# Linear attention's output pass moved into the next element's middle, with narrower key-value, numerator and score products

## The reference, cut to what matters

```python
qkv = xn @ Wqkv                     # 128 -> 3 x 1024
q, k = elu(q) + 1, elu(k) + 1       # exp below zero, t + 1 above
kv = einsum('bhnd,bhnf->bhdf', k, v)
k_sum = k.sum(axis=-2)
out = einsum('bhnd,bhdf->bhnf', q, kv) / (einsum('bhnd,bhd->bhn', q, k_sum) + 1e-6)
s = out.reshape(B, N, 1024) @ Wout + bout
```

## Time and profile before

| What | Value |
|---|---|
| median of three runs | 2235.43 us |
| profiled execution, its own time | 2234.39 us |
| its span | 2232.6 us |
| PE busy | 1934.6 us (87%), 17956 records |
| PEld busy | 1381.8 us (62%) |
| DVE busy | 1362.9 us (61%) |
| ACT busy | 1096.1 us (49%) |
| POOL busy | 214.6 us (10%) |
| mean granted TensorE clock | 0.953 |

### The profile page before, as it was taken

How to read it: one execution, slowest core, us unless ns; L and a number is a source line. 1 busy time by engine, 2 the same in 40 slices (tenths; PEclk the granted TensorE clock), 3 DMA queues, 4 the chain that set the end, 5 groups by cost and what they waited for, 6 DMA issues and landing times.

```text
span 2232.6 us, 50773 instructions
## 1 busy us (share of the span) xinstructions
PE 1934.6 (87%) x17956; PEld 1381.8 (62%) x17972; DVE 1362.9 (61%) x3678; ACT 1096.1 (49%) x2434; POOL 214.6 (10%) x235
## 2 busy tenths in 40 slices
PE   6999999998999999959888988898988899898652
PEld 4666666666666666636667566765766676666552
DVE  6666666666666666637665765577666566755312
ACT  3444444443555445425665465555555554555332
POOL 0000000000000000030011001101111110010022
PEclk9999999999999999969999999999999999999887
DMA  3222222222122211230221112110211111111374
GB/s 127 79 87 87 87 87 92 91 86 64 59 68 68 67 49 53 75 116 23 63 67 47 56 56 66 52 30 24 67 46 58 58 53 41 37 46 42 124 233 119
DMA packets 97041, 159.05 MB, mean 71 GB/s; under 512 B 14279, under 2 KB 65607, under 8 KB 93640
## 3 DMA queue, kind: packets, MB, share of 16 engines
q1 hardware_dynamic: 87720, 134.93, 18.7%
q0 software_dynamic: 9248, 23.17, 3.4%
HBM read 96.35 MB, written 61.69 MB: 71 GB/s over the span
## 4 chain that ended last, share of the span: by engine, by line
PE 59%; DVE 20%; ACT 7%; issue 7%; SPq 3%; DMA 2%; POOL 1%; another core or an unknown queue 1%; DVEq 0%; ACTq 0%; POOLq 0%
PE psum L1032 5%; PE psum L870 5%; PE psum L937 4%; PE psum L830 4%; PE psum L764 3%; PE psum L1012 3%; PE psum L987 3%; PE psum L1142 3%; PE psum L952 2%; PE psum L1090 2%; PE psum L959 2%; PE psum L786 2%; PE psum L904 2%; PE psum L1041 2%; PE psum L877 2%
## 5 line engine op out<-in xcount | busy, mean ns | idle before, releaser
L1349 ACT ACTIVATE pts<-psum 128x512 f32<-128x512 f32 x192 | 99.1, 603 | 201.1 <-PE psum L904 201.1
L1803 DVE TENSOR_REDUCE mneg<-psum 128x2 f32<-128x512 f32 (+1 forms) x192 | 119.1, 683 | 46.8 <-PE psum L885 25.1
L671 POOL DMA_INDIRECT rows<-h,recA x64 | 61.5, 961 | 894.7 <-DVE recA L1585 767.3
L786 PE MATMUL psum<-txT,wt 128*128 128x128 f32 x864 | 118.9, 281 | 32.1 <-ACT txT L1241 32.0
L786 PEld LDWEIGHTS psum<-txT,wt 128*128 128x128 f32 x864 | 106.7, 194 | 43.9 <-ACT txT L1241 38.4
L870 PE MATMUL psum<-wa,xT_s 128*128 128x512 f32 x256 | 118.0, 603 | 2.6 <-DVE mneg L1803 2.6
L1032 PE MATMUL psum<-xT_s,wa 128*128 128x256 f32 x512 | 116.6, 381 | 0.0
L695 POOL DMA_INDIRECT rows<-xn,recC x32 | 31.5, 983 | 861.5 <-DVE recC L2007 741.3
L1550 DVE TENSOR_TENSOR tg<-tg,psum 128x256 f32<-128x256 f32 x84 | 35.2, 419 | 113.6 <-ACT tg L1230 109.2
L1032 PEld LDWEIGHTS psum<-xT_s,wa 128*128 128x128 f32 x512 | 95.8, 192 | 12.9 <-issue 1.0
L795 PE MATMUL psum<-wt,tg 128*128 128x128 f32 x528 | 79.2, 280 | 14.6 <-DVE tg L1552 13.8
(11 more groups left out here) (272 smaller groups left out, 4862.7 us busy)
## 6 DMA issues: line engine op xcount, KB each, us to landing
wt<-in_wB SPq DMA_DIRECT2D x84, 384.0 KB, 2.9
outs<-pbd SPq DMA_DIRECT2D x16, 1024.0 KB, 7.2
wt<-in_wD SPq DMA_DIRECT2D x24, 578.0 KB, 3.5
wa<-in_wD SPq DMA_DIRECT2D x15, 578.0 KB, 3.6
tx<-rows SPq DMA_DIRECT2D x132, 64.0 KB, 2.9
outs<-ty SPq DMA_DIRECT2D x132, 64.0 KB, 1.6
rows<-pbd SPq DMA_DIRECT2D x64, 128.0 KB, 1.7
rows<-pbd SPq DMA_DIRECT2D x8, 1024.0 KB, 3.9
```

What stands on the lines that cost most here:

```text
L786: last = mm(bank(f"th{j}")[:, c * P:(c + 1) * P], view[s][:, c * P:(c + 1) * P], txT[:, s, :], start=True, stop=True)
L1349: af(pT[:, n, :], bank(f"e{n}"), ACT.Exp, scale=float(HD) ** -0.5).then_inc(*frees(f"e{n}"))
L1803: ins = v.tensor_reduce(mneg[:, int(n >= 4), col:col + hs], sc, AX.X, ALU.max, negate=True)
```

## The change

The products of keys with values and the numerators are computed per head: 64 weight columns and 65 moving columns for keys with values, blocks of 64 rows by 64 columns for the numerators. `kvb` halves to 65 columns, and the two heads of a pair sit in its lower and upper 64 partitions. They take two banks for four. The masks of `scores(1)` and `scores(2)` cover only the second 128 keys, and each of their products is cut into two of 128 keys.
The transposes of the linear outputs (`outputs_turned`), their copies by ScalarE and the output product s0 (`linear_output`) are no longer done at the end of the same element: they are stage G's, so they run for the element before, in the middle of the present one. In "GP" they run once more, behind the gate. `oT` moves from the keys' buffer to the one that the exponentials of the queries had. In VectorE's order the sum of s0 with the bias stands between `divided(0)` and `divided(1)`; the wait for the stored record moves to x2. The load of three layer-1 weights by SyncE waits for s0 of "GP".
Left out below: the same calls in the order for segments without A, the counts of `PER`, and the removed ScalarE helper that comes back unchanged but for its first two lines.

```diff
@@ -91,20 +91,23 @@
         names += [f"sc{n}" for n in range(4, 8)]
-        names += [f"kv{j}" for j in range(4)]
+        over("oT00", "oT01")
+        names += [f"kv{j}" for j in range(2)]
         tile_step(2)
+        over("oT10", "oT11")
         names += [f"num0{j}" for j in range(4)]
+        over("s0")
         tile_step(4)
-        names += ["oT00", "oT01", "pn0", "pd0", "oT10", "oT11"]
+        names += ["pn0", "pd0"]
         tile_step(5)
-        names += ["pn1", "pd1", "s0"]
+        names += ["pn1", "pd1"]
@@ -249,7 +251,7 @@
         reg = sb("reg", [P, 12 * 512])
-        kvb = sb("kvb", [P, NP, 2 * V0])
+        kvb = sb("kvb", [P, NP, V0])
@@ -320,7 +322,7 @@
         o_tok = big[:, 2 * INNER + NT * H * V0:].rearrange("p (t f) -> p t f", t=NT)
-        oT = big[:, 0:2 * INNER].rearrange("p (a n) -> p a n", a=NP)
+        oT = reg[:, 0:2048].rearrange("p (a n) -> p a n", a=NP)
@@ -330,7 +332,7 @@
         diag_mask = cmask[:, 1:2, :].to_broadcast([P, GR, P])
-        row_mask = cmask[:, 0:2, :].rearrange("p (o t) n -> p o (t n)", o=1).to_broadcast([P, 2, N])
+        diag_mask_2 = cmask[:, 1:2, :].to_broadcast([P, 2, P])
@@ -594,6 +596,7 @@
                     sp.wait_ge(*given("h2_ready"))
+                    sp.wait_ge(*read_out("s0"))
@@ -860,6 +863,27 @@
+            def outputs_turned(t):
+                if "G" not in now["stages"]:
+                    return
+                pe.wait_ge(*given("o_ready", t - 1))
+                for c in range(2):
+                    pe.wait_ge(*emptied(f"oT{t}{c}"))
+                    for a in range(4):
+                        last = tr(bank(f"oT{t}{c}")[:, a * P:(a + 1) * P], o_tok[:, t, (4 * c + a) * P:(4 * c + a + 1) * P])
+                    last.then_inc(*fills(f"oT{t}{c}"))
+            def linear_output():
+                if "G" not in now["stages"]:
+                    return
+                pe.wait_ge(*emptied("s0"))
+                pe.wait_ge(*read_out("oT11"))
+                for t in range(NT):
+                    for pr in range(NP):
+                        last = mm(bank("s0")[:, t * P:(t + 1) * P], oT[:, pr, t * P:(t + 1) * P], wout0[:, pr, :], start=(pr == 0), stop=(pr == NP - 1))
+                last.then_inc(*fills("s0"))
@@ -874,7 +898,10 @@
                         pe.wait_ge(*emptied(use))
-                        mm(bank(use), identb[:, :], diag_mask if part == 0 else row_mask, start=True, stop=False)
+                        if part == 0:
+                            mm(bank(use), identb[:, :], diag_mask, start=True, stop=False)
+                        else:
+                            mm(bank(use).rearrange("p (h n) -> p h n", h=2)[:, :, P:N], identb[:, :], diag_mask_2, start=True, stop=False)
@@ -882,7 +909,9 @@
                             else:
-                                last = mm(bank(use)[:, a * N:(a + 1) * N], qr[p0:p0 + HD, 2 * (part - 1) + a, P:N], kr[p0:p0 + HD, :], start=False, stop=(a == heads - 1))
+                                for kt in range(NT):
+                                    last = mm(bank(use)[:, a * N + kt * P:a * N + (kt + 1) * P], qr[p0:p0 + HD, 2 * (part - 1) + a, P:N], kr[p0:p0 + HD, kt * P:(kt + 1) * P],
+                                              start=False, stop=(a == heads - 1 and kt == NT - 1))
@@ -906,23 +935,21 @@
                     if t == 0:
-                        for j in range(4):
+                        for j in range(2):
                             pe.wait_ge(*read_out(f"kv{j}"))
+                    for hh in range(2):
+                        for c in range(2):
+                            pe.wait_ge(*emptied(f"num{t}{2 * hh + c}"))
                         pe.sem_inc(sem("tiles_open"), 1)
-                    for j in range(4):
-                        pe.wait_ge(*emptied(f"num{t}{j}"))
-                        for a in range(2):
-                            pr = 2 * j + a
-                            last = mm(bank(f"num{t}{j}")[:, a * N:a * N + 2 * V0], qt[:, pr, t * P:(t + 1) * P], kvb[:, pr, :], start=True, stop=True)
-                        last.then_inc(*fills(f"num{t}{j}"))
-                def outputs_turned(t):
-                    pe.wait_ge(*read_out(f"num{t}3"))
-                    for c in range(2):
-                        pe.wait_ge(*emptied(f"oT{t}{c}"))
                         for a in range(4):
-                            last = tr(bank(f"oT{t}{c}")[:, a * P:(a + 1) * P], o_tok[:, t, (4 * c + a) * P:(4 * c + a + 1) * P])
-                        last.then_inc(*fills(f"oT{t}{c}"))
+                            for ch in range(2):
+                                tokens = slice(t * P + ch * CH, t * P + (ch + 1) * CH)
+                                for c in range(2):
+                                    rows = slice(c * DH, (c + 1) * DH)
+                                    last = mm(bank(f"num{t}{2 * hh + c}")[ch * CH:(ch + 1) * CH, a * V0:(a + 1) * V0], qt[rows, 4 * hh + a, tokens],
+                                              kvb[rows, 4 * hh + a, :], start=True, stop=True)
+                                    if a == 3 and ch == 1:
+                                        last.then_inc(*fills(f"num{t}{2 * hh + c}"))
@@ -976,22 +1003,26 @@
                 scores(1)
+                outputs_turned(0)
                 pe.wait_ge(*read_out("v11"))
-                for j in range(4):
-                    pe.wait_ge(*emptied(f"kv{j}"))
-                    for a in range(2):
-                        pr = 2 * j + a
+                for hh in range(2):
+                    pe.wait_ge(*emptied(f"kv{hh}"))
+                    for a in range(4):
                         for t in range(NT):
-                            last = mm(bank(f"kv{j}")[:, a * N:a * N + 2 * V0], k_tok[:, t, pr * P:(pr + 1) * P],
-                                      v_tok[:, t, 2 * pr:2 * pr + 2, :], start=(t == 0), stop=(t == NT - 1))
-                    last.then_inc(*fills(f"kv{j}"))
+                            for c in range(2):
+                                hd = 2 * (4 * hh + a) + c
+                                last = mm(bank(f"kv{hh}")[c * DH:(c + 1) * DH, a * V0:(a + 1) * V0], k_tok[:, t, hd * DH:(hd + 1) * DH],
+                                          v_tok[:, t, hd, :], start=(t == 0), stop=(t == NT - 1))
+                    last.then_inc(*fills(f"kv{hh}"))
                 tile_step(2)
+                outputs_turned(1)
                 numerators(0)
+                linear_output()
@@ -1000,17 +1031,9 @@
                 tile_step(4)
-                outputs_turned(0)
                 weighted(0)
-                outputs_turned(1)
                 weighted(1)
-                pe.wait_ge(*emptied("s0"))
-                pe.wait_ge(*read_out("oT11"))
-                for t in range(NT):
-                    for pr in range(NP):
-                        last = mm(bank("s0")[:, t * P:(t + 1) * P], oT[:, pr, t * P:(t + 1) * P], wout0[:, pr, :], start=(pr == 0), stop=(pr == NP - 1))
-                last.then_inc(*fills("s0"))
@@ -1322,6 +1348,18 @@
+            def outputs_turned(t):
+                if "G" not in now["stages"]:
+                    return
+                act.wait_ge(*given("q0_ready", 1 if "A" in now["stages"] else 0))
+                act.sem_inc(sem("act_turn"), 1)
+                for c in range(2):
+                    act.wait_ge(*filled(f"oT{t}{c}"))
+                    src = bank(f"oT{t}{c}").rearrange("p (a n) -> p a n", a=4)
+                    ins = af(oT[:, 4 * c:4 * c + 4, t * P:(t + 1) * P], src, ACT.Copy)
+                    ins.then_inc(*frees(f"oT{t}{c}"))
@@ -1782,6 +1815,14 @@
+            def linear_output():
+                if "G" not in now["stages"]:
+                    return
+                dve.wait_ge(*filled("s0"))
+                v.tensor_tensor(s0[:, :, :], tok(bank("s0")[:, 0:N]), boutb[:, :].rearrange("p (o d) -> p o d", o=1).to_broadcast([P, NT, D]), ALU.add).then_inc(*frees("s0"))
+                dve.wait_ge(*read_out("s0"))
@@ -1824,17 +1865,19 @@
                             dve.wait_ge(*filled(f"num{t}{j}"))
-                            nm = bank(f"num{t}{j}").rearrange("p (a n) -> p a n", a=2)[:, :, 0:2 * V0].rearrange("p a (h v) -> p a h v", v=V0)
-                            den = dn[:, 4 * (j % 2):4 * (j % 2) + 4].rearrange("p (a h) -> p a h", a=2)
-                            v.tensor_scalar(den, nm[:, :, :, DH], 1e-6, None, ALU.add).then_inc(*signals("dve_chain"))
+                            nm = bank(f"num{t}{j}")[:, 0:4 * V0].rearrange("p (a v) -> p a v", v=V0)
+                            den = dn[:, 4 * (j % 2):4 * (j % 2) + 4]
+                            v.tensor_scalar(den, nm[:, :, DH], 1e-6, None, ALU.add).then_inc(*signals("dve_chain"))
                         for j in (2 * pair, 2 * pair + 1):
-                            nm = bank(f"num{t}{j}").rearrange("p (a n) -> p a n", a=2)[:, :, 0:2 * V0].rearrange("p a (h v) -> p a h v", v=V0)
```

(28 more changed lines are left out.)

23 lines of the change are left out of this document (12 added, 11 removed).

## The result

| What | Before | After |
|---|---|---|
| median of 19 runs each | 2238.62 us (2228.66 to 2242.86) | 2250.16 us (2236.7 to 2264.99) |
| profiled execution, its own time | 2234.39 us | 2250.16 us |
| its span | 2232.6 us | 2248.2 us |
| PE busy | 1934.6 us | 1925.0 us |
| DVE busy | 1362.9 us | 1340.8 us |

The ratio of the times is 1.0053, with a 95% interval of 1.0033 to 1.0074. The change makes the kernel some 12 us slower, where 20 us less was forecast. The 2250 us lie inside the forecast's range of 2180 to 2256, near its slow end, but the direction is the other one. TensorE has 10 us less of busy time although it works slower on average, so work was saved. The last row of the table is where to look.

The account below looks back on a forecast made before the run. TensorE's order of work, with a few stops ended by VectorE, was taken to bound the layer-0 loops. First loop -9, tiled elements -7, first element -6.5 and "GP" +2.5 made -20 us: 2214 us, range 2180 to 2256.

Parts of the forecast that it names:

- Keys with values: Layer 0's key-value products, now 64 narrower records at 33 ns: 2.1 us, 1.7 less per element.
- rival C: Narrow key-value products don't overlap in the column halves, 59 ns each: +27 us on the forecast, 2241 us; chance 0.17.
- Numerators: Per token half, 16 records become 64 quadrant records: 1.05 us for 1.9, 0.85 less, twice per element.
- The stall: Middle: VectorE idle some 3 us before the maxima's transpose, TensorE 1.9 and 1.1 us; 2 to 3.5 in the tail.
- ScalarE's open late start: Tail, first loop: ScalarE starts 1.6 us after the weighted sums, unexplained; taken as 0.1 to 1.6 us.
- The whole at full clock: Per element without clock loss: 3.8 us less in the first loop, 3.0 us less with tiles.
- The first element: No predecessor, so its transposes and output product vanish; middle 2.6 us earlier, tail 5.8 less with 2.0 open: -6.5 us.
- Clock: First loop: one fall of the old length, 1.7 us lost, plus 1.0 for the tail wait; net -1.1 per element.
- tiled elements: Elements with expert tiles: -3.0 us at full clock, +2.0 for a new clock fall, -1.0 times 7 = -7 us.
- Rival B: Output product ahead of the maxima's transpose stalls VectorE, then TensorE; two clock falls per element: +21, 2256 us; chance 0.18.
- Rival A: The clock holds, because output product and transposes fill the middle enough: -55, 2179 us; chance 0.15.
- Layer 1: The loops behind 1020 us, left aside because nothing of the diff runs there; no term in the sum.

Follow-up runs that it names:

- e4: The changed kernel with mask products that nobody reads in TensorE's three layer-0 waits (two in the middle, one before the attention output); 2195.6 us, ratio 0.9833 to before.
- e6: The changed kernel with unread mask products in its two middle waits only, the wait before the attention output left empty; 2195.2 us, ratio 0.9839 to before.
- e8: The kernel before, with unread mask products in its three middle waits; 2208.7 us, ratio 0.9886 to before.
- e9: The changed kernel with unread mask products in the wait before the last numerators alone; 2203.1 us, ratio 0.9847 to before.
- e2: The kernel before with only the narrower products (masks, keys with values, numerators), nothing moved; 2244.0 us, ratio 1.0031 to before.
- e7: The kernel before with only the narrower products, plus unread mask products in its middle waits; 2173.8 us, ratio 0.9739 to before.
- e1: The changed kernel with the output product moved behind the transpose of the row maxima on TensorE; 2206.8 us, ratio 0.9874 to before.

## Why the prediction was wrong

**Keys with values: right.** 2.1 us forecast, 2.09 measured, 33 ns per record. The weight loads have all 128 rows and alternate between column halves, and the trace has weight loads of 138 ns (median) starting every 33 ns on average, so they do overlap. By the Trainium skill (TensorE: Matmul & The Clock Gate, "The mechanism") they should not, since it allows the overlap only for other row groups. The trace disagrees, and rival C falls with it.

**Numerators: nearly.** They took 1.25 us for 1.05, so the forecast had 0.2 us too little ahead of the output product. Together with the transposes (1.09 each for 1.0) and the split scores it puts the maxima's transpose at 378.3, where the forecast's 377.2 would be 377.8 on this element's start.

**The stall: right.** VectorE idle 2.71 us for 3, TensorE 1.85 and 1.16 for 1.9 and 1.1, the tail 2.03 for 2 to 3.5. ScalarE's open late start shrank to 0.36 us: its logarithm begins at 396.78, as this row of the timeline of ACT shows, and the last weighted sums end at 395.39 + 1.03 = 396.42.

```profile
396.78 0.60 ACT L1391 ACTIVATE aden<-psum 128x512 f32<-128x512 f32 x1 [3.54 <-PE psum L964]
```

**The whole at full clock: right.** The forecast put the first loop's element 3.8 us under 54.6 when no clock is lost, 50.8. e4 reads 50.6. With tiles it put it 3.0 us under 63.9, 60.9. e6 reads 60.9. That both hit to 0.2 us is in part luck: the 3.8 was picked from 3.2 to 4.7, and 3.4 of it was the old half clock left out, so the work itself was to gain 0.4 us; at full clock it gained 0.9 (e8 to e4). The first element was forecast 6.5 us shorter with its old fall still in it. It is 52.3 us long, 3.2 shorter, and 46.1 in e9, where it has no fall. Of the 3.3 us missing from the forecast, the fall of the clock, 10.2 us long for the old 6.8, makes some 1.7 (half of the difference), and 1.0 us comes from the start of the program: the first sixteen products take 6.29 us for 5.27 before (4.82 in e9).

**The step that failed is the one called "Clock".** It took "one fall of the old length, of which half lies over time that VectorE sets anyway", 1.7 us, and 1.0 us as a share for the tail: 2.7 us per element. Both halves were off. The fall grew to 10.8 us at half clock per element, from 6.8. It hangs mostly on the wait of 1.85 us before the last numerators: with that wait alone filled (e9), 1.9 us of it are left. And hardly anything of it was covered: from after to e4 10.8 us less at half clock gave 4.6 us back, 0.42 per us where halving the speed can cost 0.5 at most, and from before to e8 6.8 us gave 3.1, 0.45 per us. The waits come ahead of the fall; what runs at half speed behind them is masks, scores and weighted sums, with TensorE busy throughout. In tiled elements 2.0 us was forecast and (322.27 - 304.59) / 5 = 3.5 measured (after to e6). So the terms read +4.7 for -9 in the first loop, and in the first element -3.2 for -6.5. The tenth element, five tiled ones and the last with "GP" together read +5.4 for -4.5. With layer 1, put at nothing and measured at +8.7 us, this is the whole distance from -20 to +15.6 us: 13.7, 3.3, 9.9 and 8.7.

**Rival B was the case that came,** by its own condition: it decides once a tiled element loses more than 3.0 us to 1.2 GHz, and it lost 3.5. That 3.5 is by e6; by e4, with its too long filling, it is 2.0. B's loss of 5 us per element was 4.6 in the first loop. Its 2256 us stand beside 2250, and part of that is luck: B put the three groups of layer 0 at +9.6, +18 and -6.5, where they read +4.7, +5.4 and -3.2, and layer 1, which it had at nothing, made up 8.7. It was given 0.18. Evidence for a longer fall lay in the rows that the forecast used: the old middle, busy 6.53 of 8.9 us, had lost 6.8 us of clock, and the change was reckoned to leave TensorE idle longer there. The tiled elements, at full clock over a wait of 1.68 us, pointed the other way. The sum then took the length of the fall from the old one. Rival A's premise, that the clock holds, was made true for layer 0's loops in e4, and the time fell with it, to 2195.6 us.

**Layer 1** was left aside because nothing of the diff runs there. That holds for its code. Its time moved by 8.7 us in the profiled pair, within what other shifts of layer 0 also do to it. In that pair the loops and single elements of layer 0 lose the other 6.9 us. How much of the 12 us between the medians is layer 1's stays open; it is measured only in the profiled executions.

## What to carry to other kernels

Before counting saved TensorE work as saved time, ask whether it leaves TensorE waiting for another engine: this kernel gave nearly all of the narrower products' gain back (e2), which was 2.3 us per element once its waits were filled (e7). In this kernel each us at half clock cost 0.4 to 0.45 us. Don't take the length of a fall over from the old kernel when the change adds waits ahead of it: here it went from 6.8 to 10.8 us. Move deferred work to where the other engine is the late one, behind what that engine waits for and not ahead of it (e1), and test a suspected clock loss by filling the waits with unread products, no longer than the wait.
